# Decoder layer on one core: values computed by tile and multiplied as f16 halves, transposes of the probabilities in another order, and the joins of the feed-forward part reordered

## What is computed

```python
def reference(x, ctx, ...):
    x = x + self_attention(layernorm(x))      # 16 heads of 128, 4 key/value heads, layernorm on q and k, rope, causal
    x = x + cross_attention(layernorm(x), ctx)  # 32 heads of 16, rmsnorm on q and k
    x = x + ffn(layernorm(x))                 # silu(x Wup) * (x Wgate), then Wdown; 512 -> 2048 -> 512, weights made ternary
    return x

def self_attention(x):
    q, k, v = split(x @ w_qkv.T)              # 2048, 512 and 512 columns
    scores = rope(norm(q)) @ rope(norm(k)).T / sqrt(128)
    weights = softmax(causal(scores))
    return (weights @ v) @ w_o.T
```

## Time and profile before

| | |
|---|---|
| median of 3 runs | 1337.52 us (1336.99 to 1341.01) |
| the profiled execution | 1341.33 us |
| its span | 1338.3 us |
| mean granted TensorE clock | 0.996 |
| busy | PE 97%, VectorE 56%, ScalarE 48%, GpSimd 22% |
| self attention | about 53 to 558 us of the span |
| cross attention | about 558 to 1050 us |
| feed-forward | about 1050 to 1338 us |

### The profile page before, as it was taken

One profiled execution on the slowest core, in us unless ns is written; L12 is line 12 of the kernel. 1 busy time (PEld: TensorE's weight loads), 2 busy tenths in 40 slices (PEclk: granted clock), 3 DMA queues, 4 the chain that ended last, 5 costly groups with the idle time before them and its releaser, 6 DMA issues.

```text
span 1338.3 us, 27069 instructions
## 1 busy us (share of the span) xinstructions
PE 1297.4 (97%) x10812; PEld 865.0 (65%) x10812; DVE 754.0 (56%) x1813; ACT 640.3 (48%) x1451; POOL 299.0 (22%) x281
## 2 busy tenths in 40 slices
PE   8989999999999999999999999999999899999998
PEld 7656666667666666566666666666666565555554
DVE  6887767777677776343444334545445883444423
ACT  4843344333533346376766776666565323222322
POOL 0853344443334451111101110111101121000000
PEclk9999999999999999999999999999999899999999
DMA  7300000000000003122222222001012300000000
GB/s 307 142 1 1 1 1 1 1 1 1 1 1 1 1 2 139 70 72 71 71 71 71 71 71 87 24 24 55 25 55 95 127 33 24 0 24 1 24 1 29
DMA packets 22892, 60.11 MB, mean 45 GB/s; under 512 B 1584, under 2 KB 11312, under 8 KB 19568
## 3 DMA queue, kind: packets, MB, share of 16 engines
q1 hardware_dynamic: 22768, 58.39, 12.3%
HBM read 55.11 MB, written 3.28 MB: 44 GB/s over the span
## 4 chain that ended last, share of the span: by engine, by line
PE 92%; DVE 3%; issue 2%; ACT 2%; POOL 0%; DVEq 0%; POOLq 0%; ACTq 0%
PE A L1711 19%; PE C L2059 12%; PE A L1615 12%; PE A L1674 10%; PE C L1742 6%; PE B L1759 5%; PE A L2078 4%; PE C L1643 3%; PE C L1658 3%; PE A L1624 3%; PE A L1692 3%; PE B L2078 2%; PE B L1635 2%; PE B L1728 2%; PE B L1651 2%
## 5 line engine op out<-in xcount | busy, mean ns | idle before, releaser
L1711 PE MATMUL A<-wxhl,arena 128*122 128x512 f16 x1152 | 265.6, 381 | 0.0
L1711 PEld LDWEIGHTS A<-wxhl,arena 128*122 128x122 f16 x1152 | 149.7, 134 | 88.7 <-issue 8.3
L1615 PE MATMUL A<-arena,wxhl 128*125 128x512 f16 (+1 forms) x780 | 173.1, 379 | 0.0
L534 POOL TENSOR_TENSOR arena<-arena,region 122x512 f32<-122x512 f32 (+2 forms) x61 | 62.9, 1061 | 414.1 <-DVE region L1169 414.1
L763 ACT ACTIVATE arena<-C 122x1600 f32<-122x1600 f32 x96 | 144.4, 1504 | 15.4 <-PE C L1742 15.4
L1615 PEld LDWEIGHTS A<-arena,wxhl 128*125 128x125 f16 (+1 forms) x780 | 104.4, 136 | 58.4 <-DVE arena L1292 0.4
L2059 PE MATMUL C<-arena 128*128 128x375 f16 (+1 forms) x768 | 138.8, 333 | 0.0
L509 POOL TENSOR_TENSOR region<-tub 125x512 f32<-125x512 f32 (+1 forms) x65 | 82.6, 1271 | 232.0 <-DVE tub L1038 232.0
L679 ACT ACTIVATE region<-C,negm 100x100 f32<-100x100 f32 x256 | 84.2, 356 | 93.6 <-DVE negm L1081 93.5
L1674 PE MATMUL A<-arena,stageb 128*125 128x512 f16 (+1 forms) x416 | 123.8, 379 | 0.7 <-ACT arena L747 0.7
L2059 PEld LDWEIGHTS C<-arena 128*128 128x128 bf16 x768 | 74.8, 97 | 58.8
(11 more groups left out here) (182 smaller groups left out, 2226.1 us busy)
## 6 DMA issues: line engine op xcount, KB each, us to landing
stageb<-in_wffn SPq DMA_DIRECT2D x16, 768.0 KB, 4.8
arena<-in_ctxt SPq DMA_DIRECT2D x16, 722.0 KB, 6.0
stageb<-in_wffn SPq DMA_DIRECT2D x8, 1024.0 KB, 6.1
arena<-in_wqkv SPq DMA_DIRECT2D x4, 1024.0 KB, 11.9
wxhl<-in_wffn SPq DMA_DIRECT2D x4, 1024.0 KB, 4.7
arena<-in_wx SPq DMA_DIRECT2D x3, 1024.0 KB, 6.9
out_x<-xres SPq DMA_DIRECT2D x12, 224.0 KB
xres<-in_x SPq DMA_DIRECT2D x1, 2560.0 KB, 12.6
```

Of the source, the lines that this page charges most:

```text
L534: pool.tensor_tensor(t, t, r, ALU.mult).then_inc(sig[done], 1)
L1615: ins = pe.matmul(A[j % 2][0:m, :], xp[:, k, at:at + m], wp[:, j, k, :], start=(n == 0), stop=(n == 11))
L1711: ins = pe.matmul(A[(par + n) % 2][0:KC, :], xp[:, k, c * KC:(c + 1) * KC], wp[:, 1 if n < 4 else 2, k, :], start=(i == 0), stop=(i == 11))
```

## The change

1. **Values by tile.** `values_of(i)` makes the values of tile i (13 in place of 16 times 12 matmuls), always in a whole turn, after `p_turn(b, 3)` and ahead of `attend(b, 2)`. ScalarE and VectorE split them into f16 halves in `vt`, and SyncE copies the rows of each batch from `vt` to one of two tiles `vvs[b % 2]` by DMA, within SBUF, since batches and tiles start at different partitions.
2. **Products from halves.** The probabilities are split too: `p_back` writes the high half, the new `p_lo` on VectorE the low half, and `attend` makes three f16 matmuls of 400 columns in place of one f32 matmul. It waits for `p_lo`.
3. **Order of transposes.** In whole turns `p_turn(b, 1)` stands ahead of `project(i, 4)`; GpSimd's `p_of` follow one each on the first four `w_of`. In attention-only turns nothing stands between `p_turn(b, 0)` and the wait for the last `z_back`.
4. **The join of cross attention and feed-forward.** `up_gate(0, 0)` goes ahead of the last `attend2`, into the A banks, and `up_gate(0, 1)` behind it; the first `hidden` goes into the last turn, a half of one ternary tile out of it, and ScalarE's dummy Silu moves behind `out_back(b, 2)`.
5. **The joins of the units.** `add_ffn(u - 1)` goes ahead of `hidden(u, 0)`; `row_scales3` is cut into four parts at e = 9 to 12; `normed3` of all tiles stands at e = 13; in units 1 and 2 `x3_lo(u + 1, 1)` moves behind `hidden_lo(u, 15)`.

The diff, cut:

```diff
+    def landed_batch(b):
+        return ld_v[b % 2], 16 * sum(c == b or (c < b and c % 2 == b % 2) for t in range(TL) for c, _, _, _ in pieces(t))
...
 # SyncE, after its first loads
+            sp.wait_ge(d_tab, 10)
+            for i in range(TL):
+                sp.wait_ge(*count("d_v", i, 1))
+                for b, lo, hi, at in pieces(i):
+                    sp.wait_ge(*count("pe_av", b - 2, 4))
+                    sp.dma_start(vvs[b % 2][lo:hi], vt[at:at + hi - lo]).then_inc(ld_v[b % 2], 16)
...
 # GpSimd, whole turn
-                for (i, j), more in zip(new, (0, 1, 2, 1, 0)):
+                for (i, j), more in zip(new, (1, 1, 1, 1, 0)):
...
 # ScalarE
+                if i > 0:
+                    for landed, total in landed_values(i - 1):
+                        act.wait_ge(landed, total)
+                act.activation(vt[0:n, 0], A[1][0:n, :], ACT.Copy, scale=SV / (SX * SW)).then_inc(sig["a_v"], 1)
...
-                act.activation(pT[:, g * 400:(g + 1) * 400], bank[0:S, 0:400], ACT.Copy)\
+                act.activation(pTh[:, g * 400:(g + 1) * 400], bank[0:S, 0:400], ACT.Copy, scale=SP)\
...
-                v_of(b + 1)
+                if new:
+                    v_of(new[0][0])
...
 # VectorE
+            def p_lo(b, g, bank):
+                dve.wait_ge(*count("a_pT", b, g + 1))
+                dve.scalar_tensor_tensor(pTl[:, g * 400:(g + 1) * 400], bank[0:S, 0:400], SP,
+                                         pTh[:, g * 400:(g + 1) * 400], ALU.mult, ALU.subtract).then_inc(sig["d_pT"], 1)
+            def v_lo(i):
+                n = rows_of(i)
+                dve.wait_ge(*count("a_v", i, 1))
+                dve.scalar_tensor_tensor(vt[0:n, 1], A[1][0:n, :], SV / (SX * SW), vt[0:n, 0],
+                                         ALU.mult, ALU.subtract).then_inc(sig["d_v"], 1)
...
 # VectorE, start
             head_norm(0)
+            v_lo(0)
             normed(1, rstd[:, 20:21])
...
 # VectorE, attention-only turn
                     back(b, 4)
                     for g in range(4):
+                        p_lo(b, g, B[(g + 1) % 2])
+                    for g in range(4):
                         a_lo(b, g)
...
 # VectorE, whole turn, behind the four proj and sums
+                p_lo(b, 0, B[0])
+                p_lo(b, 1, B[1])
+                proj(*new[4])
+                p_lo(b, 2, B[0])
+                p_lo(b, 3, B[1])
                 next_stats(b)
-                proj(*new[4])
...
                 a_lo(b, 0)
                 head_norm(new[0][0])
+                v_lo(new[0][0])
                 next_normed(b)
                 for g in range(1, 4):
                     a_lo(b, g)
...
 # VectorE, last turn
             add_attn(TL - 2, A[0])
+            p_lo(b, 0, B[0])
+            p_lo(b, 1, B[1])
             w_lo(11)
+            p_lo(b, 2, B[0])
             ctx_lo(0)
             w_lo(12)
+            p_lo(b, 3, B[1])
...
 # VectorE, feed-forward unit
-                hidden(u, 0)
                 if not first:
                     add_ffn(u - 1)
+                    hidden(u, 0)
...
                     if not first:
                         hidden_lo(u, e)
+                    if e == ET - 1 and not first and not last:
+                        x3_lo(u + 1, 1, C[1])
                     if e + 1 < ET:
                         hidden(u, e + 1)
...
+                    elif 9 <= e <= 12:
+                        scales3_part(u + 1, e - 9)
...
 # TensorE
             def attend(b, g):
-                pe.wait_ge(*count("a_pT", b, g + 1))
+                pe.wait_ge(*count("d_pT", b, g + 1))
                 if g == 0:
-                    pe.wait_ge(*count("a_v", b, 1))
-                pe.matmul(C[g][:, 0:400], vv[:, g * D:(g + 1) * D], pT[:, g * 400:(g + 1) * 400],
-                          start=True, stop=True).then_inc(sig["pe_av"], 1)
+                    pe.wait_ge(*landed_batch(b))
+                n = 0
+                for half, probs in ((0, pTh), (1, pTh), (0, pTl)):
+                    ins = pe.matmul(C[g][:, 0:400], vvs[b % 2][:, half, g * D:(g + 1) * D], probs[:, g * 400:(g + 1) * 400],
+                                    start=(n == 0), stop=(n == 2))
+                    n += 1
+                ins.then_inc(sig["pe_av"], 1)
...
 # TensorE, whole turn
                 p_turn(b, 0, B[0])
+                if b % 5 == 0:
+                    pe.wait_ge(*count("d_pT", b - 1, 4))
+                p_turn(b, 1, B[1])
                 pe.wait_ge(*count("d_u", i, 3))
                 project(i, 4)
-                p_turn(b, 1, B[1])
                 attend(b, 0)
-                pe.wait_ge(*count("a_pT", b, 1))
                 p_turn(b, 2, B[0])
                 attend(b, 1)
-                pe.wait_ge(*count("a_pT", b, 2))
                 p_turn(b, 3, B[1])
+                pe.wait_ge(*count("d_u", i, 4))
+                values_of(i)
                 attend(b, 2)
                 attend(b, 3)
-                pe.wait_ge(*count("d_u", i, 4))
-                values_of(b + 1)
...
 # TensorE, attention-only turn
                 p_turn(b, 0, B[1])
-                if x is not None:
-                    pe.wait_ge(*count("d_xlo", x, 1))
-                else:
-                    pe.wait_ge(*count("a_v", b, 1))
-                values_of(b + 1)
                 pe.wait_ge(*count("d_zT", i, 5))
                 p_turn(b, 1, B[0])
                 attend(b, 0)
-                pe.wait_ge(*count("a_pT", b, 1))
+                pe.wait_ge(*count("d_pT", b, 1))
                 p_turn(b, 2, B[1])
...
 # TensorE, last turn of the cross attention
                 attend2(b, 2, par)
                 if end < 2:
                     scores2(b + 1, 0)
+                else:
+                    up_gate(0, 0, True)
                 attend2(b, 3, par)
                 if end == 2:
+                    pe.wait_ge(*count("a_e", b, NU))
+                    up_gate(0, 1, True)
                     pe.wait_ge(*count("d_on", o2_tile(b), 1))
```

More of the change, by code:

```diff
@@ L343, in build, with hidden_banks @@
         C = [Call[:, i * 512:(i + 1) * 512] for i in range(4)]
+        def hidden_banks(u, e):
+            return A if u == 0 and e == 0 else C[2 * (e % 2):2 * (e % 2) + 2]
         ld_c, ld_c2 = sem("ld_c"), sem("ld_c2")
@@ L349, in build @@
         ld_x0 = sem("ld_x0")
+        ld_v = [sem(f"ld_v{n}") for n in range(2)]
         ld_x = sem("ld_x")
@@ L411, in build, with landed_values @@
         block = ctx.enter_context(nc.Block())
+        def landed_values(i):
+            n = [0, 0]
+            for t in range(i + 1):
+                for b, _, _, _ in pieces(t):
+                    n[b % 2] += 16
+            return list(zip(ld_v, n))
+        def landed_batch(b):
+            return ld_v[b % 2], 16 * sum(c == b or (c < b and c % 2 == b % 2) for t in range(TL) for c, _, _, _ in pieces(t))
         @block.sync
@@ L573, in _ @@
             pool.wait_ge(*count("pe_qk", TL - 1, 5))
-            pool.wait_ge(*count("pe_v", NB - 1, 1))
+            pool.wait_ge(*count("pe_v", TL - 1, 1))
             pool.memset(ctxs[:, :, CTX:CTXP], 0.0).then_inc(g_zero, 1)
@@ L1220, in row_stats3, with scales3_part @@
                     st.did(dve.bn_stats(stats3[0:n, r], xres[0:n, i, :]))
-            def row_scales3(u):
+            def scales3_part(u, part):
+                t = len(unit_tiles(u))
+                if part > 0:
+                    if part == 1:
+                        rsqrt_start(rs3[:, 0:t], ms3[:, 0:t])
+                    st.chain(rsqrt_step(rs3[:, 0:t], ms3[:, 0:t], t))
+                    return
                 st.wait()
-                t = len(unit_tiles(u))
                 st.did(dve.tensor_copy(statc3[:, 0:t], stats3[:, 0:t]))
@@ L1232, in row_scales3 @@
                 st.chain(dve.tensor_scalar(ms3[:, 0:t], mv3[:, 0:t, 1], EPS_LN, SX ** -2, ALU.add, ALU.mult))
-                st.chain(rsqrt(rs3[:, 0:t], ms3[:, 0:t], t))
+            def row_scales3(u):
+                for part in range(4):
+                    scales3_part(u, part)
             def normed3(u, r):
@@ L1506, in turn @@
                     add_cross(o2_tile(b), 1)
-                if end == 2:
-                    ternary(5, 1)
-            for b in range(NB):
-                turn(b, b % 2, max(0, b - NB + 3))
             def hidden(u, e):
@@ L1548, in unit @@
             def unit(u, first=False, last=False):
-                hidden(u, 0)
                 if not first:
                     add_ffn(u - 1)
+                    hidden(u, 0)
+                tiles = [] if last else range(len(unit_tiles(u + 1)))
                 for e in range(ET):
@@ L1554, in unit @@
                         hidden_lo(u, e)
-                    if first:
-                        if e < 12:
-                            ternary(6 + e // 2, e % 2)
-                        if e in (1, 3, 5):
-                            row_stats3(u + 1, (e // 2,))
+                    if e == ET - 1 and not first and not last:
```

(43 more changed lines are left out.)

93 lines of the change are left out of this document (50 added, 43 removed).

## The result

After the change the kernel takes **1343.8 us** (median of 14 runs), and before it 1339.9 us over as many runs (the 1337.5 of the table above is the median of three): ratio **1.0027**, 95% interval 1.0016 to 1.0038. So it is slower by about 0.3%. The profiled execution took 1344.35 us with a span of 1342.3, that is 4.0 us more than the span before. One of the four executions of a later kernel, s9_best, took 2209.08 us at a mean granted clock of 0.557, and its ratio is taken over the other three.

The account below looks back on a forecast made before the run. TensorE, with 92% of the chain of waits, was taken to bound the kernel. Attention +17.7, join -6.1 and units -5.6 gave +6.0 on 1341.33, 1347.3; less 3.8 this is 1343.5 us against 1337.52, range 1330 to 1350.

Parts of the forecast that it names:

- TensorE's own work: Attends and values: 0.70 to 0.51 us over 64 attends, -12.2, and fewer value matmuls, -7.8; together -20.0 if nothing waits.
- The rival that the halves save nothing: At 0.57 us or more an attend, waits hide the difference, adding 1 to 2 us; 0.09 together with the clock rival.
- The wait for p_back(1) behind square(4): Ordinary whole turns: p_lo(1) waits for ScalarE's copy until 255.24, part of a VectorE chain 2.4 us later; turn 1.1 longer.
- VectorE does that behind v_lo (0.6) and the next normed tile (1.29): Six whole turns: a_lo(1) comes late, so the output projection's second group is 2.1 us later, 2.3 in batches 2, 7, 12.
- The first turn: Batch 0: four p_lo less cheaper statistics move head_norm by 1.7 us and, with v_lo, z_back by 2.3: +2.3.
- Rival C: Last turn's 3.3 us gap: TensorE's clock could fall, costing 3 to 4 us, total 1347; 0.09 together with the halves rival.
- The last turn: p_lo(2) ahead of ctx_lo makes TensorE wait 3.3 us at the context's first projection; following block starts +3.4 later.
- the join: Cross attention to feed-forward: up_gate moved into the wait, clock at 1.00, -6.1 us; -3.5 if the clock still falls.
- the units: Idle time ahead of down products goes, -6.4, and unit 2 loses 0.8: together -5.6 us, between -3 and -6.4.
- The three attention-only turns: Batches 4, 9, 14: copy, p_lo and attend wait in a row; -1.3 us each, -4.0, of 3.4 each taken out.
- The last step, from the profiled execution to the median: Whole kernel: 3.8 us subtracted because the profiled execution stood over the median, turning 1347.3 into 1343.5 us.
- Rival B: Head transpose of whole turns: chain at most 1.4 us later, waits covered, 1321 us, half way 1327 to 1333; chance 0.24.

Follow-up runs that it names:

- s9_best: s5_stats with first-turn weight 9's low half on GpSimd ahead of its gain, scaled on ScalarE ahead of square 4, and batch 0's VectorE reordered: 1322.52 us, ratio 0.9871.
- s2_swap: The changed kernel with ScalarE's p_back(b, 1) ahead of the square of projection 4 in whole turns: 1336.46 us, ratio to before 0.9980.
- s10_attn: The changed kernel with the join and the unit order taken back, so only self attention differs from before: 1355.2 us, ratio to before 1.0119.
- s5_stats: The changed kernel with ScalarE's swap, new VectorE orders in first and last turn, and next tile's statistics moved behind projection 0: 1323.37 us, ratio to before 0.9879.
- s1_seam: The kernel before with only the join of cross attention and feed-forward and the unit order changed: 1328.07 us, ratio to before 0.9921.
- s6_order: The changed kernel with next_normed ahead of v_lo on VectorE instead of behind it: 1347.01 us, in a single execution.

## Why the prediction was right, and where it wasn't

The mechanism was right: TensorE's work was saved and came back as waits, slower by some 0.3%. Over the attention stage 22.2 us were saved and the stage is 16.4 longer, so 38.6 came back (said 37.7): 22.9 are listed waits, 3.4 the clock of the first two turns, and the rest, by difference, lies in what the list leaves out. Point by point:

- **TensorE's own work.** An attend went from 0.70 to 0.51 as said; the last two of a turn, which run back to back, from 1.54 to 1.02. So it is 0.90 a batch and not 0.76: the term was 2 us too small. The rival that the halves save nothing is refuted.
- **The wait for p_back(1) behind square(4)** was right in place and size, and s2_swap shows it as the cause: 0.8 us a turn in eleven turns. The head transpose's wait came at 0.81 (said 0.9), and turns 5 and 10 at +1.12 (said +1.1).
- **"VectorE does that behind v_lo (0.6) and the next normed tile (1.29)"** is the step that failed. The 1.36 us of the row couldn't be carried over: the same operation took 0.76 us, since the 1.36 held a wait for GpSimd's first operation. v_lo fits in under that wait, so a_lo(1) came 0.6 us earlier: +1.5 to +1.6 instead of +2.1 to +2.3 in six turns, 3 to 4 us in all. The same step gave the start +0.6 and it was 0: there too the normalised rows end 1.32 us behind GpSimd's start, in before and in after.
- **The first turn.** +2.3 was said; in s10_attn, where the clock holds until 80 us (it is 0.72 from 80 to 86), it is 34.68 - 32.21 = +2.5. The wait ahead of attend 0, behind weight 9 on VectorE, isn't in the prediction, and its clock cost 1.9 us more in that turn and 1.5 in the next in the profiled execution. Rival C put the fall into the last turn's gap; there the clock stayed at 1.00 from 536 to 546 us, through an idle time of 3.09.
- **The last turn** (+3.3, said +3.4), **the join** (-6.3, said -6.1, with the clock at 1.00 through it) and **the units** (-6.1, said -5.6) hold. The three attention-only turns gained 1.4 to 1.5 of the 3.5 us taken out, as said. No wait of TensorE for the values' DMA was found.
- **The last step, from the profiled execution to the median,** was wrong by as much as the sum: the net was +4.0 and not +6.0, but I took 3.8 off for an execution that stood over the median of three runs. Over 14 runs before's median is 1339.9, so it stood 1.5 over it, and after's profiled run stands 0.6 over its own. That 1343.5 met 1343.8 so closely is in part luck: two errors of opposite sign, 2.0 and 2.3 us.
- **Rival B** needed the chain no more than 1.4 us later. s5_stats makes that state: swap and statistics take some 1.9 us out of the chain, and 1323.4 us stand against that rival's 1321. But the total agrees for other reasons than the rival's. It had the eight whole turns 7.2 us shorter than before; they are 2.1 shorter, and the last turn (+0.5 in place of +3.4) and turns 3, 8 and 13 (-1.8 in place of 0) bring what is missing.

Even then the arithmetic doesn't arrive whole. Against s1_seam, s5_stats gains 4.7 us in the medians (0.42% in the ratios), where some 22 were taken out of TensorE. A whole turn keeps 0.1 to 0.5 of its 0.9; 2 of 3.5 us are lost in each attention-only turn, where copy, low half and attend wait for each other in a row; and the first turn is still 2.6 longer than before.

## What to carry to other kernels

When the engine that sets the time gets less to do, look for the helper's chain that fed it, and for the position of each input of that chain in its own engine's order: one copy that stood behind one square cost 0.8 us in eleven turns, and two lines gave it back. Test the parts of a change apart; here a net of +4 us was -11 and +15. Before a duration is carried from a row to another order of work, see what ran beside it: 1.36 us were 0.76 as soon as another operation stood first.

## What the hardware showed that I had not expected

- VectorE's TENSOR_SCALAR from SBUF to SBUF stood while GpSimd's TENSOR_TENSOR ran: 0.17 us became 0.46, 0.82, 2.97 and 3.71, each ending 0.03 to 0.04 us behind GpSimd's end. The low half of weight 9, with two sources in SBUF, took 2.96 us in before and in after, where it overlaps a product of GpSimd by 0.8 us, and those of the last turn, of the same shape and without GpSimd beside them, 2.29. Operations with one source in PSUM weren't held: v_lo took 0.69 us beside GpSimd in after and 0.68 in s6_order. Nor was the sum of squares (TENSOR_REDUCE), with 0.67 us in s9_best beside GpSimd's 4.08. The Trainium skill (SBUF — State Buffer, SBUF: two separate sides) calls the port pair that VectorE and GpSimd share an exclusive lock, which an operation of VectorE in a two-port mode or, against a GpSimd operation that reads SBUF, with two sources in SBUF, or one of GpSimd, holds for its whole length; whichever starts first gets it. The first part agrees with these rows. The second can't be read off the records: in s6_order VectorE's began 0.04 us ahead of GpSimd's first and still took 1.37 us. That is one distance of start times, and spans of GpSimd are rough.
- It works the other way too: beside the 2.96 us of weight 9's low half on VectorE, GpSimd's product of the probabilities took 2.90 us in before and in after (0.85 otherwise). It began 0.8 us into VectorE's operation and ended 0.7 us behind its end.
- With the same idle time of TensorE in the first turn (3.21, 3.21 and 3.22 us) the granted clock of the window from 70 to 75 us was 0.73, 0.91 and 1.00, in three executions with the same order of work up to there; with 3.90 us it was 0.84, and behind 3.09 us in the last turn 1.00. A single profile can't price such a gap, nor prove its mending.
